# Two attentions of a decoder: scores, looks and value products sent in twos

## The reference, cut to what matters

```python
# stage 7, the memory attention: 8 heads of 16, 1601 keys
Q = _split_heads(query, H) * depth ** (-0.5)
k_mem, v_mem = jnp.split(memory, 2, axis=2)
logits = jnp.einsum('bhqd,bhkd->bhqk', Q, K) + b[0]
logits = logits + -1e+30 * (1.0 - mask)
weights = jax.nn.softmax(logits, axis=-1)
out = jnp.einsum('bhqk,bhkd->bhqd', weights, V)
# stage 10, the cross-self attention: 16 heads of 8, 1601 + 256 keys
k = jnp.concatenate([extra_k, k], axis=2)
v = jnp.concatenate([extra_v, v], axis=2)
attn = jnp.einsum('bhnd,bhmd->bhnm', q * scale, k).astype(jnp.float32)
attn = jax.nn.softmax(attn, axis=-1).astype(dtype)
out = jnp.einsum('bhnm,bhmd->bhnd', attn, v)
```

## Time and profile before

| what | number |
| --- | --- |
| time, median of 3 runs | 4901.98 us (4900.62 to 4909.86) |
| the profiled execution, time | 4901.46 us |
| its span, first to last instruction | 4899.7 us |
| mean granted TensorE clock | 0.888 of 2.4 GHz |

### The profile page before, as it was taken

The page is one execution under the profiler, slowest core; times in us unless marked ns, Lnnn a source line. Parts: engine busy times, 40 slices in busy tenths (PEclk is TensorE's granted clock), DMA queues, the critical chain, the costliest instruction groups (busy, mean ns, idle before and its releaser), DMA issues. The chain is left out here.

```text
span 4899.7 us, 76840 instructions
## 1 busy us (share of the span) xinstructions
PE 4014.5 (82%) x29259; PEld 2239.6 (46%) x29259; DVE 3459.8 (71%) x5343; ACT 2437.2 (50%) x3285; POOL 1335.5 (27%) x984
## 2 busy tenths in 40 slices
PE   5640978999999999999959986848995768888883
PEld 3630445666666666666633333423443432222232
DVE  5468556878787788878764455757764658888868
ACT  2120225666666666666642233535662446777672
POOL 0000003666666666666657012000000100000000
PEclk6565989999999999999979997969995779999996
DMA  0010610000000000000013026325540433223300
GB/s 19 1 54 1 127 40 28 14 1 14 1 14 1 14 6 10 14 1 1 1 60 135 0 61 121 42 55 81 80 58 4 105 73 59 47 45 53 49 2 9
DMA packets 145923, 183.98 MB, mean 38 GB/s; under 512 B 21562, under 2 KB 110156, under 8 KB 144932
## 3 DMA queue, kind: packets, MB, share of 16 engines
q1 hardware_dynamic: 137860, 162.65, 16.3%
q0 software_dynamic: 6528, 16.42, 1.4%
q10 hardware_dynamic: 1184, 0.12, 0.0%
HBM read 141.04 MB, written 35.08 MB: 36 GB/s over the span
## 5 line engine op out<-in xcount | busy, mean ns | idle before, releaser
L3002 POOL TENSOR_TENSOR arena<-arena 128x512 f32<-128x512 f32 (+1 forms) x768 | 1133.1, 1477 | 630.8 <-ACT arena L2956 577.1
L2449 ACT ACTIVATE arena<-ps 128x1024 f32<-128x1024 f32 (+1 forms) x688 | 703.3, 1023 | 327.0 <-PE ps L2374 316.3
L2467 DVE TENSOR_REDUCE arena<-ps 128x2 f32<-128x826 f32 (+1 forms) x576 | 564.8, 980 | 175.2 <-PE ps L2320 167.4
L3018 DVE TENSOR_TENSOR arena<-arena 128x1024 f32<-128x1024 f32 (+1 forms) x448 | 652.8, 1496 | 35.0 <-ACT arena L2985 35.0
L3040 DVE TENSOR_TENSOR arena<-ps,arena 128x512 f32<-128x512 f32 (+1 forms) x768 | 530.3, 690 | 109.2 <-ACT arena L2950 75.8
L2320 PE MATMUL ps<-arena 48*128 48x413 bf16 (+3 forms) x1920 | 433.8, 332 | 131.5 <-DVE arena L2467 67.9
L2950 ACT ACTIVATE arena<-ps 128x1024 f32<-128x1024 f32 (+1 forms) x448 | 410.6, 960 | 200.6 <-PE ps L2878 194.8
L2956 ACT ACTIVATE arena<-arena 128x1024 f32<-128x1024 f32 (+1 forms) x448 | 425.0, 992 | 60.1 <-DVE arena L3018 57.6
L2393 PE MATMUL ps<-arena 128*9 128x256 f32 (+2 forms) x5504 | 433.4, 387 | 10.8 <-ACT arena L2437 8.0
L2878 PE MATMUL ps<-arena 64*128 64x256 f32 (+1 forms) x3328 | 427.4, 391 | 5.9 <-ACT arena L2972 1.3
L2892 PE MATMUL ps<-arena 128*64 128x256 f32 (+1 forms) x3328 | 412.7, 388 | 5.8 <-ACT arena L2956 5.8
(11 more groups left out here) (641 smaller groups left out, 5609.4 us busy)
## 6 DMA issues: line engine op xcount, KB each, us to landing
arena<-ctx_parts SPq DMA_DIRECT2D x96, 200.1 KB
arena<-ctx_parts SPq DMA_DIRECT2D x192, 100.1 KB
arena<-fs_rows SPq DMA_DIRECT2D x128, 128.0 KB, 4.0
arena<-in_ctx_feat SPq DMA_DIRECT2D x8, 1601.0 KB, 6.5
arena<-in_ctx SPq DMA_DIRECT2D x16, 768.0 KB
arena<-diff_att_stack SPq DMA_DIRECT2D x60, 192.0 KB
ctx_parts<-arena SPq DMA_DIRECT2D x24, 400.2 KB, 3.4
arena<-in_w SPq DMA_DIRECT2D x1, 6416.0 KB, 19.0
```

The source lines that it names most:

```text
L2449: act.activation(self.prob[0:rows, u % 3, :], self.ps[0:rows, 2 * (u % 2):2 * (u % 2) + 2, :].rearrange("p n c -> p (n c)"), ACT.Exp).then ...
L2467: ins = dve.tensor_reduce(dst[:, :, j // 2], self.ps[:, 4:6, 0:hi - lo], AX.X, ALU.max)
L3002: pool.tensor_tensor(acc[0:rows, u % 2, :], before, sc[0:rows, u % 2, t, :], ALU.add).then_inc(added, 1)
L3018: dve.tensor_tensor(e, e, mb[0:rows, u % 2, None, :].to_broadcast([rows, n, 2 * S]), ALU.subtract).then_inc(sub_done, 1)
```

## The change

Three things change, in both stages. The steps of a group are taken by twos: PE sends two scores in a row and two value products in a row, and the looks of two steps stand half before and half behind the value products (`values_at` says which products come at which step: at an even step of a group those of the two steps before). The maxima's turn and the results' turn are sent right behind a look at two heads, at the first even look not before the place that they had (`turn_at`, `back_at`), on PE and DVE alike, and ACT copies the maxima at the step in which that look is sent (`rows_at`). The ring of exponentials has four places; to make room in stage 10, the remainders of queries and keys (`rest_qk`) use two of them before the attention starts.

```diff
-        self.prob = st.sb("prob", [P, 3, 4 * S])
+        self.ring = 4
+        self.prob = st.sb("prob", [P, self.ring, 4 * S])
...
+        total = self.groups * self.looks
+        pair_from = lambda n: n + n % 2
+        self.turn_at = {pair_from(self.looks_by(2 * self.turn_step(g) + 2)): g for g in range(1, self.groups)}
+        self.back_at = {pair_from(self.looks_by(2 * self.back_step(g) + 1)): g for g in range(self.groups - 1)}
+        self.rows_at = {self.look_step(n): g for n, g in self.turn_at.items() if n < total}
+        self.late_turns = {self.turn_step(g): g for n, g in self.turn_at.items() if n >= total}
+        self.late_backs = {self.back_step(g): g for g in range(self.groups - 1)
+                           if pair_from(self.looks_by(2 * self.back_step(g) + 1)) >= total}
...
+    def look_step(self, n):
+
+        return next(u for u in range(self.groups * self.steps)
+                    if u % self.steps % 2 == 0 and self.looks_by(2 * u + 2) > n)
+
+    def back_step(self, g):
+
+        return (g + 1) * self.steps + 2
...
+    def values_at(self, u):
+
+        t = u % self.steps
+        if t % 2:
+            return []
+        if t:
+            return [u - 2, u - 1]
+        return list(range(u - (self.steps - 1) % 2 - 1, u)) if u else []
...
-                            self.prob[0:rows, u % 3, k % 2 * 2 * S + k // 2 * S:k % 2 * 2 * S + k // 2 * S + S],
+                            self.prob[0:rows, u % self.ring, k % 2 * 2 * S + k // 2 * S:k % 2 * 2 * S + k // 2 * S + S],
...
     def run_pe(self, pe):
         total = self.groups * self.steps
-        turns = {self.turn_step(g): g for g in range(1, self.groups)}
-        backs = {(g + 1) * self.steps + 2: g for g in range(self.groups - 1)}
         self.turned = self.backed = 0
         pe.wait_ge(self.sem["ones_loaded"], 4 * 2 * 16)
+
+        def look(n):
+            self.pe_look(pe, n)
+            if n in self.turn_at:
+                self.pe_turn_max(pe, self.turn_at[n])
+            if n in self.back_at:
+                self.pe_back(pe, self.back_at[n])
         for n in range(self.looks):
-            self.pe_look(pe, n)
+            look(n)
         self.pe_turn_max(pe, 0)
         for n in range(self.looks, self.looks_by(0)):
-            self.pe_look(pe, n)
+            look(n)
+        done = self.looks_by(0)
         for u in range(total):
             self.pe_scores(pe, u)
-            for n in range(self.looks_by(2 * u), self.looks_by(2 * u + 1)):
-                self.pe_look(pe, n)
-            if u:
-                self.pe_values(pe, u - 1)
-            for n in range(self.looks_by(2 * u + 1), self.looks_by(2 * u + 2)):
-                self.pe_look(pe, n)
-            if u in turns:
-                self.pe_turn_max(pe, turns[u])
-            if u in backs:
-                self.pe_back(pe, backs[u])
-        self.pe_values(pe, total - 1)
+            if u % self.steps % 2 == 0:
+                end = self.looks_by(2 * u + 2)
+                for n in range(done, (done + end + 1) // 2):
+                    look(n)
+                for v in self.values_at(u):
+                    self.pe_values(pe, v)
+                for n in range((done + end + 1) // 2, end):
+                    look(n)
+                done = end
+            if u in self.late_turns:
+                self.pe_turn_max(pe, self.late_turns[u])
+            if u in self.late_backs:
+                self.pe_back(pe, self.late_backs[u])
+        for v in self.values_at(total):
+            self.pe_values(pe, v)
         self.pe_back(pe, self.groups - 1)
...
     def run_act(self, act):
         s = self.sem
         total = self.groups * self.steps
-        turns = {self.turn_step(g): g for g in range(1, self.groups)}
         self.act_rows(act, 0)
         for u in range(total):
             act.wait_ge(s["st_ready"], u + 1)
-            if u >= 3:
-                act.wait_ge(s["pv_done"], u - 2)
+            if u >= self.ring:
+                act.wait_ge(s["pv_done"], u - self.ring + 1)
             rows = self.tiles[u % self.steps][1]
-            act.activation(self.prob[0:rows, u % 3, :], self.ps[0:rows, 2 * (u % 2):2 * (u % 2) + 2, :].rearrange(
+            act.activation(self.prob[0:rows, u % self.ring, :], self.ps[0:rows, 2 * (u % 2):2 * (u % 2) + 2, :].rearrange(
                 "p n c -> p (n c)"), ACT.Exp).then_inc(s["exp_done"], 1)
             if u and u % self.steps == 0:
                 self.act_take(act, u // self.steps - 1)
-            if u in turns:
-                self.act_rows(act, turns[u])
+            if u in self.rows_at:
+                self.act_rows(act, self.rows_at[u])
+            if u in self.late_turns:
+                self.act_rows(act, self.late_turns[u])
         self.act_take(act, self.groups - 1)
...
         total = self.groups * self.steps
-        backs = {(g + 1) * self.steps + 2: g for g in range(self.groups - 1)}

         def look(n):
             self.dve_look(dve, n)
             if n % self.looks == self.looks - 1:
                 self.dve_split(dve, link, n // self.looks)
+            if n in self.back_at:
+                self.dve_out(dve, link, self.back_at[n])
         for n in range(self.looks_by(0)):
             look(n)
+        done = self.looks_by(0)
         for u in range(total):
-            for n in range(self.looks_by(2 * u), self.looks_by(2 * u + 2)):
-                look(n)
-            if u in backs:
-                self.dve_out(dve, link, backs[u])
+            if u % self.steps % 2 == 0:
+                for n in range(done, self.looks_by(2 * u + 2)):
+                    look(n)
+                done = self.looks_by(2 * u + 2)
+            if u in self.late_backs:
+                self.dve_out(dve, link, self.late_backs[u])
         self.dve_out(dve, link, self.groups - 1)
...
-            rest_qk = sa.sb("rest_qk", [P, 4, BANK])
+            rest_qk = att.prob[:, 0:2, :].rearrange("p r (h c) -> p (r h) c", c=BANK)
```

## The result

The changed kernel takes 4919.22 us (median of 18 runs, 4911.74 to 4936.42) against 4901.76 for the kernel before (18 runs, 4890.67 to 4916.23): a ratio of 1.0034, 95% interval 1.0024 to 1.0044. It is slower by about 17 us; 4936 was forecast. The profiled execution has a span of 4913.7 us, 14.0 more than that of before.

What follows compares the result with a forecast made beforehand. PE was taken to set stage 7's pace, and the waits between PE and DVE stage 10's. From 4901.46 us, +41 (stage 10), -11 (stage 7) and +5 (maxima) gave 4936 us, range 4888 to 4962.

Steps and rivals of the forecast that it cites:

- looks that wait for their one place: Both attentions: one pair of banks for looks at two heads, so at least 1.47 us from one to the next.
- the look behind the results: Stage 10, step 4: this look waits 1.25 us for bank 7 while DVE reads and makes results; two value products stand behind.
- stage 10's groups, 29 of them: Cross-self attention: PE waits grow 2.85 us against 1.4 saved, +1.4 us a group, +41 us in all.
- stage 7's groups: Memory attention: PE saves 1.2 us, waits grow 0.4, so 0.8 us gained a group, -11 us over 14 groups.
- maxima for the next group: Stage 10: the later turn leaves the maxima's transfers 2.9 us for 4.69, so more come late: +5 us.
- 22.56 against 21.17: Stage 10: laid-out length of a group in us, new order against old, giving +1.4 us a group.
- near 22.8: Stage 10: group length in us expected in the profile after, 22.56 + 0.3.
- Value products: Both stages: two in a row take 0.99 us to what follows; each that joins another saves 0.20 us of PE.
- rival (b): No change: joined value products run faster, at the lower bound 0.22, waits grow about 1.8 us: 4904 us, chance 0.08.
- Rival (a): Faster: PE's drains bound both stages and waits don't grow, so 59 us gained: 4843 us, chance 0.12.
- Rival (c): Slower still: maxima late in most groups, transfers queued behind loads, 13 to 25 us above forecast, about 4957; chance 0.16.
- DVE's waits: Stage 10: DVE's waits for looks, on L2467's line, up by over 1 us a group; PE's for DVE by nearly 3.

Runs made afterwards that it cites:

- e1: Scores and value products in twos and the new turns in stage 7 alone, stage 10 in the old order: 4881.21 us, 0.9951 of the kernel before.
- e3: The changed kernel with scores and value products in twos, but both turns at their old places: 4906.21 us, 4904.9 for the kernel before.
- e6: Twos with turns at their old places, and DVE reading only the last eighth of each look's columns: 4795.31 us, 4901.19 for the kernel before.
- e5: The kernel before, with DVE reading only the last eighth of each look's columns, in both stages: 4842.05 us against 4901.19.

## Why the prediction was right or wrong

Right were the direction, the mechanism and its sign in each stage: looks that wait for their one place, the look behind the results standing over a microsecond (1.01, longest 1.2), stage 7 gaining while stage 10 loses more. The size was too large by 17 us. By terms of the sum:

| term | forecast | measured |
| --- | --- | --- |
| stage 10's groups, 29 of them | +41 | 29 x 1.08 = +31.3 |
| stage 7's groups | -11 | 13 x 0.88 = -11.4, and -6.6 for POOL's copies, -1.2 in the last two |
| maxima for the next group | +5 | about +4 |

**The step that failed** is "22.56 against 21.17": the +1.4 a group was the layout of after less the layout of before. The first came out well: 22.54 measured. The second was 0.3 short of the trace, 21.46, and the prediction said so itself, then took the 0.3 for something that both orders share and even wrote that groups would be near 22.8. Measured against the trace, 22.56 - 21.46 = 1.10 would have been the term, 32 us, and the forecast 4927.

What the layouts missed can be estimated. The layout counts a stand from the moment at which the next piece could have started; the profile counts it from the end of the last matmul's row, 0.07 (a value product) to 0.17 us (a look) later. With these ends added, the seven stands of the group before are 3.4 us (2.51 in the profile, 3.66 laid out) and the eleven of the group after 6.2 (4.42; 6.5 laid out). What is left of each group, PE's work, is 18.0 before for 17.5 laid out, and 16.4 after for 16.1. So the waits rose by 2.7 for 2.85, and the work fell by 1.6 for 1.4. Both layouts lacked work of PE; in that of after, waits laid out 0.3 too long made up for it, so its 22.56 is in part luck. Which piece of PE's work was priced too low is open.

**Stage 7** is the other term of the wrong size, -11 for -19. Its groups came out at 21.52, the forecast's "near 21.6". What was missed is that four slow groups of before had a cause that depends on where POOL's copies fall. They were in the trace, but the forecast took the undisturbed group times the number of groups, in stage 7 without a word on the others. This part of the gain is chance: the change shifts the splits against the copies, it doesn't part them; in e1 one group met a copy, in e3 five did.

**Value products** cost what was said: from 4324.39 to 4325.37 two take 0.98, for 0.99. That excludes rival (b) with its 0.22, and with waits that grow by only 1.8. From one look at two heads to the next, where PE stands for it, it is still 1.47 (4322.15 to 4323.62). **Rival (a)** fell with e3 for stage 10; e6 shows what it needs: without DVE's long reads twos do gain there, by 0.14, and in stage 7 by 1.56. **Rival (c)** did not come. The maxima are copied and first needed at these times after, the answer to the earlier trace rows, and the waits for them stand below, the answer to the earlier trace rows:

```profile
4333.62 0.26 ACT L2467 ACTIVATE arena<-ps 24x128 bf16<-24x128 f32 x1
...
4336.93 0.47 PE L2392 MATMUL ps<-arena 51*128 51x256 bf16 x4
```

```profile
PEld ps L2392 <- DMA arena<-arena: 13.8, 9, 3.8
```

From the end of the copy 3.05 us are left, for 4.69 before and 2.9 laid out; nine are late for seven, by 3.9 us more in all.

**DVE's waits** for looks rose from 53.3 to 96.0 us, 1.4 a group, as forecast ("over 1"), but not on L2467's line, which fell a little (52.9 to 48.0): the single looks (L2508, L2512) are late now, being sent behind a look at two heads that itself waits. PE's waits for DVE rose by 1.7 a group as the profile counts them, not by nearly 3.

## What to carry to other kernels

Work out a change of order against the trace, not against a layout of the old order: where the layout misses the old time, that miss need not be a constant to be taken along. Sending like operations together pays on an engine that has the most work and costs where its partner must be fed evenly through a single buffer; the same edit can have both signs in two stages of one program, and then belongs in one of them. Look at the groups that are slower than the rest before counting groups: they have a cause of their own, and a change may remove it or bring it back by accident.

## What the runs showed of the hardware

**POOL's copy holds DVE.** A DVE instruction of 0.17 us whose operands lie in SBUF took up to 1.47 us when POOL's copy had begun first, and ended with it (3426.37, above); DVE's reads of looks from PSUM beside such copies kept their time (0.90 in stage 7, 1.02 in stage 10). The Trainium skill, page "SBUF — State Buffer", section "SBUF: two separate sides", says that DVE and GpSimd share a port pair as an exclusive lock, held for the whole instruction by the one that starts first, among DVE's for those in a 2-port perf mode or with two SBUF inputs. The tensor_tensor at 3609.14 in before, two SBUF inputs, 1.47 us, agrees with it; the cast at 3426.37 has one input, and no run here shows in which mode it ran.

```profile
3609.14 1.47 DVE L2488 TENSOR_TENSOR arena<-arena 128x8 f32<-128x8 f32 x1
```

**Late maxima cost more than their wait.** PE's stand for one late transfer in stage 10 of before, by windows (granted clock is the third number from the end):

```profile
4418.00:4426.00 8.00, 7.45 (x86) 2.40 (x86) 7.42 (x11) 5.71 (x7) 0.00 (x0) 1.00 0.86 132
4426.00:4429.20 3.20, 0.11 (x2) 0.00 (x1) 0.84 (x2) 0.00 (x0) 0.00 (x0) 0.81 0.53 133
4429.20:4438.00 8.80, 8.80 (x63) 2.48 (x65) 4.48 (x7) 4.45 (x5) 2.05 (x3) 0.50 0.01 4
4438.00:4446.00 8.00, 6.71 (x83) 2.22 (x83) 7.28 (x14) 6.14 (x6) 0.00 (x0) 0.99 0.01 2
```

PE stands for 3.1 us, the clock falls meanwhile, and for the next 8.8 us it is granted at 0.50, 1.2 GHz: 63 matmuls, where the 8 us ahead held 86. In e5, where groups of 18.5 leave the transfers less time, 13 groups wait for their maxima, 43.1 us in all:

```profile
PEld ps L2374 <- DMA arena<-arena: 43.1, 13, 6.6
```

Going by e5, the transfers of the maxima would have been next, had the change made stage 10's groups shorter.

**Two exponentials in a row** on ACT take 1.94 us, not twice 1.02, as in this row of the timeline after:

```profile
4316.74 1.94 ACT L2485 ACTIVATE arena<-ps 128x1024 f32<-128x1024 f32 x2
```

The prediction laid them out at 1.02 and 0.02 between; that only widens ACT's idle time, which was not the bound.
